# A ring of twelve places for the experts' weights, the shared expert's last features packed into whole products, and two steps moved, in a Transformer layer with 60 experts on one core

## What is computed

```
x: [2, 1024, 256]; 16 query heads, 4 key heads of 64 features
x = x + attention(layernorm(x)) @ out_kernel          # softmax over 1024 keys, no mask
y = layernorm(x)
gu = y @ se_gate_up_w.T                                 # 2 x 704 features
shared = silu(gu[:, :704]) * gu[:, 704:] @ se_down_w.T * sigmoid(y @ shared_gate_w.T)
weights, sel = top_k(softmax(y @ gate_w.T), 4)          # 60 experts
for e in range(60):                                     # w13 [352, 256], w2 [256, 176]
    gu_e = y @ w13[e].T
    sparse += cw[:, e] * (silu(gu_e[:, :176]) * gu_e[:, 176:]) @ w2[e].T
out = x + shared + sparse                               # 2048 rows
```

## Time and profile before

| | |
|---|---|
| three runs | 740.02, 741.34, 733.32 us (median 740.02) |
| the profiled execution | 737.07 us |
| its span (first to last instruction) | 735.3 us |
| TensorE busy | 678.1 us, 92% |
| VectorE, ScalarE, GpSimd busy | 438.7 (60%), 502.0 (68%), 320.2 us (44%) |
| bytes moved | 75.91 MB, mean 103 GB/s |
| expert stage, first pair of tiles with both neighbours | 486.54 us |
| last pair's start | 711.56 us |

### The profile page before, as it was taken

The page is one execution under the profiler, slowest core; times in us unless marked ns, Lnnn a source line. Parts: engine busy times, 40 slices in busy tenths (PEclk is TensorE's granted clock), DMA queues, the critical chain, the costliest instruction groups (busy, mean ns, idle before and its releaser), DMA issues.

```text
span 735.3 us, 18110 instructions
## 1 busy us (share of the span) xinstructions
PE 678.1 (92%) x5691; PEld 357.2 (49%) x5691; DVE 438.7 (60%) x1215; ACT 502.0 (68%) x847; POOL 320.2 (44%) x400
## 2 busy tenths in 40 slices
PE   8789999999999999998899999899997978988996
PEld 6623333434434343436687887444443433444542
DVE  6864543556634464526778535667775755656758
ACT  3687878788898888872223223588886876886981
POOL 4652434244222265336204545456554553554333
PEclk9999999999999999999879999999998998999998
DMA  6000000000022000029201222177775866776686
GB/s 188 2 1 1 1 1 1 1 1 30 30 53 96 30 30 1 30 62 222 40 30 4 73 66 80 52 222 223 229 226 162 249 201 173 221 201 195 195 296 209
DMA packets 43022, 75.91 MB, mean 103 GB/s; under 512 B 7944, under 2 KB 23756, under 8 KB 42932
## 3 DMA queue, kind: packets, MB, share of 16 engines
q1 hardware_dynamic: 33556, 53.81, 24.8%
q0 software_dynamic: 9376, 20.97, 9.7%
HBM read 58.07 MB, written 16.67 MB: 102 GB/s over the span
## 4 chain that ended last, share of the span: by engine, by line
PE 75%; DVE 13%; issue 5%; another core or an unknown queue 1%; DVEq 1%; DMA 1%; SPq 1%; ACT 1%; ACTq 0%
PE p_o L1930 17%; PE p_gu L2108 13%; PE p_s L1918 11%; PE p_y L2131 8%; PE p_xs L2092 2%; PE p_hT L2118 2%; PE bench L1849 2%; PE p_d L2032 2%; PE bench L1836 2%; PE p_d L2034 1%; PE p_d L2033 1%; PE bench L1944 1%; PE bench L1966 1%; PE bench L1982 1%
## 5 line engine op out<-in xcount | busy, mean ns | idle before, releaser
L1069 ACT ACTIVATE probs<-p_s 128x1024 f32<-128x1024 f32 x256 | 243.6, 1034 | 46.4 <-PE p_s L1918 44.8
L974 ACT ACTIVATE placed<-ring 88x512 f32 x237 | 138.9, 626 | 13.7 <-PE p_d L2034 9.1
L1694 DVE COPY placed<-ring 128x704 f32 x237 | 120.1, 534 | 47.0 <-issue 24.9
L1930 PE MATMUL p_o<-probs,vext 128*32 128x512 f32 x1024 | 137.0, 608 | 0.5 <-DVE enr L1319 0.5
L949 POOL DMA_INDIRECT expert_out<-ys,goes_to x79 | 84.4, 1068 | 77.3 <-ACT ys L974 46.4
L2108 PE MATMUL p_gu<-ring,xsT 128*32 x316 | 107.0, 483 | 5.9 <-issue 5.4
L2108 PE MATMUL p_gu<-placed,xsT 128*32 128x352 f32 x948 | 107.7, 484 | 0.0
L1918 PE MATMUL p_s<-qst,kst 64*128 64x512 f32 x512 | 95.5, 449 | 3.9 <-DVE kst L1504 2.2
L920 POOL DMA_INDIRECT xs_low<-x_rows,choice_i x64 | 63.6, 994 | 69.1 <-PE p_gu L2108 32.4
L866 POOL DMA_INDIRECT members<-place,slot x48 | 47.0, 978 | 100.9 <-PE p_o L1930 83.6
L2131 PE MATMUL p_y<-placed,hT 88*32 88x256 f32 x948 | 82.7, 386 | 1.6 <-issue 1.5
(11 more groups left out here) (299 smaller groups left out, 1199.5 us busy)
## 6 DMA issues: line engine op xcount, KB each, us to landing
ring<-in_w_dram SPq DMA_DIRECT2D x60, 352.0 KB
ring<-in_w_dram SPq DMA_DIRECT2D x60, 176.0 KB
plane<-expert_out SPq DMA_DIRECT2D x10, 512.0 KB
x_rows<-rows SPq DMA_DIRECT2D x4, 520.0 KB, 3.4
x2T_kept<-xt SPq DMA_DIRECT2D x3, 512.0 KB, 2.8
x2r<-x2T_kept SPq DMA_DIRECT2D x3, 512.0 KB, 7.6
sup<-in_sup_dram SPq DMA_DIRECT2D x2, 704.0 KB, 6.2
expert_out<-ys,goes_to POOLq DMA_INDIRECT x79
```

The lines of the kernel that those rows point to most:

```text
L974: return nc.scalar.activation(o, i_, ACT.Copy, **kw)
L1069: nc.scalar.activation(probs[:, j % NPB, :], p_s[j % NSB][:, :], ACT.Exp, scale=SCALE)\
L1694: last = v.tensor_copy(placed13[:, i % N13, h, :], ring[:, bass.ds(ring_at(tile, h), W13)])
L1930: last = mm(p_o[32 * g_:32 * g_ + 32, :], vext[c // 2][:, kb, rr // 2 + KP * h, :], probs[:, (2 * u + half) % NPB, h * QC:(h + 1) * QC], s ...
```

## The change

Four edits.

1. The ring has twelve places, and the extra four stand where parts of the attention's and the shared expert's buffers were. Expert e has place (e + 4) mod 12. The first four experts are loaded where eight were, the next four after the last rows are stored, the four after them when the shared expert's last product is through. Gate and up weights and down weights are now two kinds of load with semaphores of their own (`w13_loaded`, `w2_loaded`, each shared by every fourth expert), two announcements (`w13_arrived`, `w2_arrived`) and two conditions: a place's gate and up part is free when TensorE has multiplied with it (`gu_in_psum`), its down part when the tile is done. Gate and up loads run six experts ahead of down loads. The loop holds twelve experts, 24 loads, and is passed three times. The first block's weights are not copied, so `placed13` and `placed2` have three places for a tile instead of four.
2. The shared expert's last 64 gate features and last 64 up features lie side by side and fill one product's 128 output rows: six products in place of twelve. Its down weights stand twice, one copy under the other, and `shT_h` holds the high part in its first 64 rows and the low part in the other 64: two products in place of three.
3. GpSimd's subtraction `sdown_l` waits for step 104 of 128 of the second sequence.
4. In `after`, each of the two turns of the last rows stands one `gu` later.

`wo` and the gate's weights are counted on one semaphore, and `tile_words` has one operation more.

```diff
@@ constants, and the order of the last rows' jobs
-    RING = 8
+    RING = 12
+    EARLY = 8
+    LATE = RING - EARLY
     RELAY = 2
+    LEAD = 6
+    NSLOT = 4
...
-                 ("gu", 0, 3), ("ln2c", C3, 0), ("gu", 0, 4), ("x2T", C3, 0), ("gu", 0, 5), ("x2T", C3, 1),
-                 ("gu", 1, 0), ("route", C3, 0), ("route2", C3, 0), ("route2", C3, 1), ("down", 0, 0),
+                 ("gu", 0, 3), ("ln2c", C3, 0), ("gu", 0, 4), ("gu", 0, 5), ("x2T", C3, 0), ("gu", 1, 0),
+                 ("x2T", C3, 1), ("route", C3, 0), ("route2", C3, 0), ("route2", C3, 1), ("down", 0, 0),
@@ SyncE
+            def relay_gate_up(at, before=0):
+                sp.wait_ge(w13_loaded[at % NSLOT], (at // NSLOT + 1) * 16 + before)
+                sp.sem_inc(w13_arrived, 1)
...
-            for e in range(RING):
-                load_expert(e, e)
+            for e in range(NSLOT):
+                load_gate_up(e, e)
+                load_down(e, e)
             sp.wait_ge(x2_split, 2)
             load_x2T(2, x2r)
             store_rows(3)
-            for e in range(RING - RELAY):
-                relay(e, e)
+            for e in range(NSLOT, EARLY):
+                relay_gate_up(e - NSLOT)
+                load_gate_up(e, e)
+                relay_down(e - NSLOT)
+                load_down(e, e)
...
+            sp.wait_ge(sdown_in_psum, NT)
+            for e in range(EARLY, RING):
+                load_gate_up(e, e)
+                load_down(e, e)
...
+            def next_gate_up(e, at, before=0):
+                free_at = sp.value_load(cnt_i[0:1, 3, bass.ds(e - RING, 1)], min_val=1, max_val=NTILE + 1)
+                sp.wait_ge(gu_in_psum, free_at)
+                load_gate_up(e, at)
+                relay_gate_up(at - RELAY, before)
+
+            def next_down(e, at, before=0):
                 free_at = sp.value_load(cnt_i[0:1, 3, bass.ds(e - RING, 1)], min_val=1, max_val=NTILE + 1)
                 sp.wait_ge(tiles_done, free_at)
-                load_expert(e, s)
...
+                load_down(e, at)
+                relay_down(at - RELAY, before)
...
             with sp.Fori(0, NR, 1) as j:
-                for s in range(RING):
...
-                    refill(j * RING + RING + s, s)
+                for e in range(RING, 2 * RING):
+                    next_gate_up(j * RING + (e + LEAD), e + LEAD, j * (RING // NSLOT * 16))
+                    next_down(j * RING + e, e, j * (RING // NSLOT * 16))
@@ GpSimd
             pool.wait_ge(sdown_high, 1)
...
+            pool.wait_ge(probs_used, 3 * SPC + 8)
+            g.tensor_tensor(sdown_l[:, :, :], sdown[:, :, :], sdown_h[:, :, :].bitcast(fp32), ALU.subtract)\
+                .then_inc(sdown_split, 1)
             pool.wait_ge(x2r_loaded[0], 16)
@@ VectorE
                 dve.wait_ge(h_high, n + 1)
-                v.tensor_tensor(shT_l[0:pf, f, :], sh[0:pf, f % 3, :], shT_h[0:pf, f, :].bitcast(fp32),
+                low_ = shT_l[:, f, :] if f < NFS - 1 else shT_h[FS_LAST:P, f, :]
+                v.tensor_tensor(low_, sh[0:pf, f % 3, :], shT_h[0:pf, f, :].bitcast(fp32),
                                 ALU.subtract).then_inc(h_split, 1)
@@ TensorE
+                if f == NFS - 1:
+
+                    to, both = p_g[pair(n)][:, :], slice(2 * f * P, 2 * FS)
+                    for k in range(KC):
+                        x_high, x_low = x2h[c % 2][:, k, :], x2l[c % 2][:, k, :]
+                        mm(to, sup_h[:, k, both], x_high, start=(k == 0), stop=False)
+                        mm(to, sup_h[:, k, both], x_low, start=False, stop=False)
+                        last = mm(to, sup_l[:, k, both], x_high, start=False, stop=(k == KC - 1))
+                    last.then_inc(sgu_in_psum, 1)
+                    return
```

More of the change, by code:

```diff
@@ L178, in attention_moe_block @@
         cnt = low("cnt", [P, 9, E])
[L179 removed]
+        eid = low("eid", [P, 12 * PER])
         slot_i = low("slot_i", [P, PER], i32)
@@ L590, in ring_at @@
         def ring_at(tile, h):
-            return ((tile >> (3 * h)) & (RING - 1)) * WE
+            return nc.s_assert_within((tile >> (4 * h)) & 15, 0, RING - 1, skip_runtime_bounds_check_because=
+                                      "a tile's word is made of places in the ring, below RING") * WE
         def wait_apart(eng, semaphore, count):
@@ L699, in tiles_out @@
+            for e in range(E - RELAY, E):
+                relay_gate_up(e)
+            for e in range(E - LEAD, E):
+                next_down(e, e)
+            for e in range(E - RELAY, E):
+                relay_down(e)
             def tiles_out(count):
@@ L1557, in of_blocks @@
                 return eid[:, n * PER:(n + 1) * PER]
-            block_no, passed, real, whose, begins, inside, row_, row_or_none, slots, two, four = map(of_blocks, range(11))
+            block_no, passed, real, whose, begins, inside, row_, row_or_none, slots, two, four, rounds = map(of_blocks, range(12))
             def blocks():
```

164 lines of the change are left out of this document (88 added, 76 removed).

## The result

| | before | after |
|---|---|---|
| median of 20 runs each | 737.49 us (731.82 to 742.91) | 729.94 us (725.99 to 733.15) |
| ratio after to before | | 0.9911, 95% interval 0.9892 to 0.993 |
| the profiled execution's span | 735.3 us | 728.5 us |
| attention's last product ends | 326.71 | 336.69 |
| the first tile's products start | 464.37 | 469.76 |

The change makes the kernel 0.9% faster. I had forecast 723 us, 14 less than the profiled execution before; between the medians it is 7.5 us less. The time lies inside the range of 706 to 732, but the change has only half of its forecast size, and the ring's term is the one that is off. The spans differ by 6.8 us, which go by stage: attention +10.0, from there to the first tile -4.6, the first pairs +0.7 (22.17 us before, 22.91 after), the 35 intervals -12.3, the end -0.6.

A forecast was written before the change was run, and what follows sets the result against it. The chain was on TensorE nearly everywhere, with 18.1 us lost where VectorE waits for SyncE's late announcements. 735.3 + 9 - 2 - 3 - 18.1 = 721.2 us of span, plus 1.8, gave 723 us; range 706 to 732.

The forecast's parts named there:

- the ring's term: Expert stage: with twelve places all 18.1 us lost at the stalls are gained; bounds 9 and 20 us.
- The stalls and their cause: Expert stage: VectorE's weight copies wait 18.6 us for SyncE, because weights are announced late, not transferred late.
- the forecast's pace: Expert stage: 5.91 us for a pair of tiles, from ten undisturbed intervals, carried over all 35.
- Twelve places: Expert stage: expert e is announced once expert e - 10 is through; four more experts give over two pairs of slack.
- Attention: Attention stage: GpSimd's later subtraction holds VectorE's small operations and TensorE stands some 7 us; loss 9 us, bounds 0 and 11.
- The 2 us for a half clock: Attention stage: 2 us added to the loss because TensorE runs at half its clock after the long wait.
- The shared expert: Shared expert's stage: packed products gain 3.0 us and a vanishing VectorE wait 2 us.
- The 2 us for a wait: Shared expert's stage: VectorE's 2.48 us wait at 344.20 may go when four experts load there instead of eight; gain 2 us.
- The sum of 3.0 for the products: Shared expert: fewer gate, up and down products gain 0.4 - 0.2 + 1.4 + 1.4 = 3.0 us; bounds 1.5 and 5.
- two terms of 0.4: Shared expert, chunk 0: gate and up moved ahead of the first turn gain 0.4 us, down products 0.4 us.
- SyncE: Expert stage: two steps per expert at 1.57 us are 3.1 us, against 3.5 us an expert lasts, so it fits.
- Rival 3: Expert stage: SyncE becomes the bound and the kernel slower, end near 755 us at 2.4 us a step; chance 0.06.

The follow-up runs named there:

- after_sub_early: The changed kernel with GpSimd's subtraction sdown_l back in its earlier place (no wait for step 104): 683.47 us, ratio 0.9792 to the kernel before.
- after_trace: The changed kernel itself, unaltered, run once more for its trace on a chip of the second kind: 687.60 us, ratio 0.982 to the kernel before.

## Why the prediction was wrong

- **The stalls and their cause: right.** The announcement held VectorE back, not the transfer. Small loads left the waits (15.5 us), and an announcement one expert earlier halved them.
- **The size of the ring's term: this step failed.** "I take all of the 18.1 us, since from 488 to 548 us the same work runs at 5.91 with the transfers it needs at that pace". The stage gained 12.3, since the intervals run at 6.08 and not at 5.91; even the same first ten take 60.46 us instead of 59.11. By phase, the 5.8 us that are missing are 1.5 of pauses (19.5 measured, 18.0 in the forecast's pace) and 4.8 in the turns of the hidden features and the gate and up products (9.6 and 4.8), less the 0.5 of the last interval. The two are hard to part: in the third interval before, a pause of 0.5 us in the row turns goes with 0.4 us in the turns of the hidden features behind it. Why the changed kernel has more of both stays open. One trace of it again on this kind gave 17.4 us of pauses and 11.2 of the rest, and all six kernels without long stalls there have 17 to 20 and 8 to 11, with full loads and with small ones.
- **What the prediction did not see in the pace.** 5.91 is not TensorE's work: it is 5.26 us and a pause of some 0.8 us in four of five pairs. The sum of the pauses rose from 12.4 to 19.5 us because the stalls had hidden some of them. In the seven intervals that had stalled, the kernel before had 1.7 us of pauses and the changed one 4.8; in the other 28, 10.7 and 14.7. Their places say the same. Counted in TensorE's products from the first of the 35 intervals (72 a pair), the traces of the first kind have their pauses, over the first 28 pairs, near 133, 211, 277 and 355, and again every 360 products; here and there one is missing and a neighbour is twice as long. In the kernel before, those near 853, 931, 1357, 1435 and 2011 have no pause of their own, and all five lie in the seven stalled intervals. That a stall covers a pause is read from this, not shown by a run of its own. The forecast's pace of 5.91 had allowed for it without my knowing.
- **What was not in the profile.** On the second kind of chip the same two kernels have no pauses, the ring is worth 16.35 us, and the time's ratio in one run each is 0.982; my 723 to 737 is 0.981. That the forecast fits there is luck in part: the ring's 18.1 came from a pace of 5.91 us that this kind of chip does not have (its first ten intervals take 5.27 us each before the change).
- **Twelve places: wrong credit.** I gave the gain to four more experts of distance. Used as eight, the stage gains all but 1 us of what it gains in the changed kernel (186.32 against 185.11 on the second kind; the full ring with the subtraction early has 186.23 there). Of the rest, 6.3 us come from refilling gate and up after their products instead of after the tile (192.60 to 186.32). 8.9 us (201.46 to 192.60, the clock's share included) belong to what else is new in the ring, the separate loads and counts and the twelve experts loaded ahead of the loop; no run separates these.
- **Attention: right.** +9 forecast, +9.98 measured, by the mechanism and operations named; the wait of 7 us is 7.22. The 2 us for a half clock behind it are there too: the granted clock is 0.50 from 297 to 301 us, and the delay against the kernel before grows from 7.7 us at the transposes to 9.98. The Trainium skill's rule on the shared port (SBUF — State Buffer, section SBUF: two separate sides) agrees with the rows of that stretch: the held operations are held to GpSimd's end, for 1.18, 0.94, 2.24 and 6.06 us. What I missed is that the unmoved subtraction would also have cost, 5.5 us at the end of attention in after_sub_early.
- **The shared expert: 5 forecast, 4.6 measured, by luck in part.** The 2 us for a wait that was to go with half of the early loads fell: it is 2.45 us with four experts loading. The sum of 3.0 for the products also leaves out one of its two terms of 0.4. Of the 4.6 us, 1.7 are there at the table's product and 2.9 behind it. No run has the packed products alone, so that they gave all of it is not shown.
- **SyncE: right.** Rival 3 did not come; VectorE's weight copies wait 0.4 us for it in the stage (2.4 us in after_trace).
- **The basis: harmless.** I took the profiled execution, 737.07 us; the median of 20 is 737.49.

## What to carry to other kernels

The pace of an undisturbed stretch is not the floor of the work. Take the interval apart by phase, find the shortest of each, and ask what stands above it and whether stalls elsewhere hide the same thing; then carry over each part by itself. Before more buffers are bought, look at which event the announcement and the refill wait for: on the second kind of chip, one constant gave 1.7% of the kernel, and another semaphore in one wait 6.3 us of the stage. An operation of GpSimd that works between SBUF tensors has to be placed between VectorE's chains of small operations, and where two such operations become one, the gap between them goes.

## What the runs showed of the hardware

- **The same program took 737 us on some chips and 697 on others**, with the same instructions. Of the 37 us between the spans of the kernel before on either kind, 23.6 are in the 35 intervals (225.02 and 201.46), 4.2 in the first pairs and 8.3 between the end of attention and the first tile; attention ends at 326.7 and 327.4.
- **TensorE's pauses.** On the first kind there is one for each 210 to 265 of its products and weight loads (5034 in the stage of either kernel, 19 to 24 pauses). Most make their interval 0.7 to 1.1 us longer, and they are put down to "issue". They come at the same products of its program in the kernel before, in the changed one and with small loads. The page's DMA part for 500 to 690 us of the changed kernel shows the instruction queue (packets, MB, share of 16 engines):

```profile
q8 instruction: 19, 0.31, 0.7%
```

That is 16 KB a packet, and about as many packets as pauses. The Trainium skill (Runtime: NRT & Kernel Launch, section Instruction fetch mechanics) says that an engine takes its program in blocks of 16 KiB, 256 instructions, and that crossing into the next is mostly hidden. The size of the packets fits, and the count and the fixed places in the program fit roughly. If the pauses are these crossings, they are hidden on the second kind, where the same program has none, and cost 17 to 20 us of this stage on the first. No run shows that, and why the kinds differ stays open: over the 35 intervals the queue moves 22 packets in 0.7 to 0.8% of the time on both.
- **VectorE beside GpSimd.** Four-column operations of 0.16 us took 0.94 to 6.06 us and ended with GpSimd's; statistics over 256 columns took 1.40 us beside GpSimd and without it.
